# Feed-forward gate and linear blocks in three rounded passes, one rotated buffer, scale and shift on ScalarE, and new instruction orders in a six-layer attention stack

## The chip, the cores and the metric

The kernel runs on one core of one Trainium2 chip. The metric is the device time of one execution in microseconds (us). Engines are named as in the profile: PE is the matmul engine (PEld its weight loads), DVE the vector engine, ACT the activation engine, POOL GpSimd, SP the engine that issues the DMAs.

## The reference

`x` holds 128 sequences of 32 tokens with 128 features. A state-space block (`_L0_cond_ref`, not touched) gives the input of six layers, and the result of the six layers is added to `x`. A layer, with `shift` moving the second half of the features one token later:

```
y = shift(x) @ Wqkv                 # 128 -> 3 x 1024: q, k, v of 16 heads of 64
q, k = l2norm(q), l2norm(k)         # per head, times q_scale / k_scale
q, k = q*cos*s + rot(q)*sin*s, k*cos/s + rot(k)*sin/s
p = softmax(8 * q @ k.T, causal)    # 32 tokens of one sequence
x = x + (p @ v) @ Wo
n = layernorm(shift(x)) * g + b
a, gate = split(n @ W1 + b1)        # 341 columns each
x = x + (a * gelu(gate)) @ W2 + b2
```

## The kernel before

The 4096 tokens are 32 tiles of 128 tokens; four tiles are a group of 512 tokens, so a layer has 8 groups and the six layers 48. The residual `res` stays on chip as 128 features x 4096 tokens. Five instruction streams, one for each engine, are written by hand as a `body` that handles one group in four steps j = 0..3; semaphores join them. `group_steps` (L666) unrolls groups 0 and 1 of a layer and loops over groups 2 to 7. The work is staggered over the steps: in step n an engine works on projections and rotation of tile n, on transposes, key placement and `copy_v` of tile n-1, on scores and softmax of tile n-2, and on the weighted values of tile n-3. `project_out` of a group runs in step 3 of the next group, and the feed-forward of a group (`subtract_mean`, `variance`, three `gate_block`s, three `a_block`s, `down`) in steps 0 to 2 of the group after that.

Products with large weights are made in three passes over operands that are split in two rounded (fp32r) parts, high and low: high x high, high x low, low x high. The parts are made by an ACT copy to fp32r (`round_part` L1113, `round_wo` L1108, `copy_oT` L1039) and a subtraction on DVE or POOL (`rest_of_part`, `rest_of_wo`, `rest_of_outputs` L1253). The feed-forward blocks (L914, L925), the transposes (L819) and `down` (L932) work on plain fp32, and such a matmul of 512 columns stands in the trace as two instructions.

The order of a step on each engine is that of its `body`: PE L935, ACT L1122, DVE L1281, POOL L1403, SP L759. The parts that matter here:

- A query or key tile is squared by ACT into `sq` (L976, L983) and summed by DVE (`sum_squares` L1179). DVE multiplies it with cosine (`times_cos` L1186) and sine (L1195), POOL adds the two into `qk_r` (`rotate` L1347) and multiplies keys with the inverse norm (`norm_keys` L1356), PE transposes (L819), and ACT copies the transposes out of `px` (`copy_qT` L1023, `copy_kT` L1030). `qk_r` has two buffers, by the parity of the tile.
- `px` in PSUM is shared by both transposes and the weighted values, so `weigh_values` (L873), and the mask fill in front of it (L843), wait for `copy_kT`. `pg` is shared by all products of the feed-forward and by `project_out`.
- The feed-forward of a group: PE L896, ACT square and copy (L1087, L1094), PE L903, ACT logarithm and exponential (L1100, L1106), DVE `normalise` (L1243) at the end of step 0 and `scale_shift` (L1250) at the start of step 1. In step 1 three `gate_block`s alternate with `gate_gelu` (L1053), between two activation table loads (L1060). `gated` (L1235) of block k waits for `a_block` k, and `a_block` k+1 waits for it.
- At the end of a group's attention DVE adds `project_out` to the residual (`add_attention` L1267), ACT copies it shifted into `fs` (`shift_ffn` L1079), and only then comes ACT's `copy_oT` (L1045), for which DVE's `rest_of_outputs` (L1257) waits.
- In group 1 of a layer ACT rounds `Wo` in step 0 (L1111), and POOL makes its low part (`rest_of_wo` L1368) at the end of step 0.

## Time and profile before

| | us |
|---|---|
| median of 3 runs | 2977.76 (2974.36 to 2978.22) |
| profiled execution, own time | 2975.6 |
| its span, first to last instruction | 2973.8 |
| busy: PE / DVE / ACT / POOL | 2805.6 / 2630.3 / 2170.5 / 2129.8 |
| granted PE clock, mean | 0.984 |

The busy time of PE is a union of records whose ends are modelled; starts are the safer reading. The first 400 us are the state-space block and the start of the first layer; the last 50 us are the drain of the last groups and the final addition.

### The profile page before, as it was taken

How to read it: one execution, taken by the hardware profiler on the slowest of the kernel's cores; microseconds unless marked ns; L12 is line 12 of the kernel's file. 1: busy time of each engine (PE TensorE's matmuls, PEld its weight loads, DVE VectorE, ACT ScalarE, POOL GpSimd, SP SyncE). 2: the span in 40 equal slices, each digit the busy share in tenths (PEclk: the TensorE clock that was granted, in tenths of full speed). 3: DMA queues.
4: the chain of work that ended last, by engine and by line, in shares of the span. 5: the costliest groups of instructions: out<-in, count | busy, mean ns of one | idle time of the engine just before them, and what ended most of it. 6: DMA issues, size and time to landing. Idle time of an engine off the chain costs nothing. (4 is left out here: it accounts for less than half of the span.)

```text
span 2973.8 us, 90541 instructions
## 1 busy us (share of the span) xinstructions
PE 2805.6 (94%) x35360; PEld 2069.6 (70%) x35360; DVE 2630.3 (88%) x3407; ACT 2170.5 (73%) x3499; POOL 2129.8 (72%) x1523
## 2 busy tenths in 40 slices
PE   8799978999999999999999999999999999999986
PEld 7688856776767676666767667676667767676762
DVE  7899968999998998989999899999999898999982
ACT  5688857777777877777787777777687777768761
POOL 6776767777777777777777777777877777777760
PEclk9899999999999999999999999999999999999997
DMA  1000022222223222222222222222232322222222
GB/s 52 22 1 1 1 52 65 66 73 66 65 64 76 66 66 69 64 73 67 72 66 62 67 73 70 68 67 64 65 74 65 74 66 58 70 64 62 58 64 61
DMA packets 103837, 178.36 MB, mean 60 GB/s; under 512 B 29222, under 2 KB 52836, under 8 KB 103524
## 3 DMA queue, kind: packets, MB, share of 16 engines
q1 hardware_dynamic: 102500, 174.69, 23.7%
q8 instruction: 116, 1.90, 0.3%
q10 hardware_dynamic: 1152, 1.20, 0.1%
q14 instruction: 69, 0.57, 0.1%
HBM read 22.72 MB, written 2.10 MB: 8 GB/s over the span
## 5 line engine op out<-in xcount | busy, mean ns | idle before, releaser
L1347 POOL TENSOR_TENSOR spare<-spare,qk_t 128x1024 f32<-128x1024 f32 x384 | 909.6, 2390 | 29.1 <-POOL xs_lo L1333 8.1
L1356 POOL TENSOR_TENSOR spare<-spare,inv 128x1024 f32<-128x1024 f32 x192 | 366.6, 1909 | 329.9 <-ACT inv L1015 326.2
L791 PE MATMUL pa<-w_hi,xs_hi 128*128 128x512 f32 x1152 | 552.7, 480 | 10.5 <-DVE w_lo L1317 5.6
L1179 DVE TENSOR_REDUCE ss<-sq 128x16 f32<-128x1024 f32 x384 | 461.0, 1200 | 29.2 <-ACT sq L976 28.3
L1186 DVE TENSOR_TENSOR spare<-pa,rot 128x1024 f32<-128x1024 f32 x384 | 465.5, 1212 | 0.0
L1195 DVE TENSOR_TENSOR qk_t<-pa,rot 128x1024 f32<-128x1024 f32 x384 | 465.4, 1212 | 0.0
L791 PE MATMUL pa<-w_hi,xs_lo 128*128 128x512 f32 x1152 | 455.8, 396 | 0.0
L791 PE MATMUL pa<-w_lo,xs_hi 128*128 128x512 f32 x1152 | 454.4, 394 | 0.0
L819 PE MATMUL px<-ident_sb,spare 128*128 128x128 f32 x3072 | 410.3, 277 | 38.2 <-ACT qT L1023 32.3
L819 PEld LDWEIGHTS px<-ident_sb,spare 128*128 128x128 f32 x3072 | 339.7, 140 | 113.9 <-POOL spare L1356 59.0
L1363 POOL TENSOR_TENSOR sm<-sm,inv 128x512 f32<-128x512 f32 x192 | 201.3, 1048 | 258.0 <-DVE sm L1217 258.0
L1257 DVE TENSOR_TENSOR oT_lo<-px,oT_hi 128x1024 fp32r<-128x1024 f32 x192 | 228.6, 1191 | 120.9 <-ACT oT_hi L1045 120.8
L1030 ACT COPY k_both<-px 128x1024 f32<-128x1024 f32 x192 | 194.9, 1015 | 134.8 <-PE px L819 130.4
L791 PEld LDWEIGHTS pa<-w_hi,xs_hi 128*128 128x128 f32 x1152 | 218.3, 189 | 99.6 <-issue 57.9
L791 PEld LDWEIGHTS pa<-w_lo,xs_hi 128*128 128x128 f32 x1152 | 218.8, 190 | 76.1 <-issue 44.0
L983 ACT ACTIVATE sq<-pa 128x1024 f32<-128x1024 f32 x192 | 199.1, 1037 | 78.1 <-PE pa L791 76.1
L976 ACT ACTIVATE sq<-pa 128x1024 f32<-128x1024 f32 x192 | 196.8, 1025 | 80.3 <-PE pa L791 74.4
L791 PEld LDWEIGHTS pa<-w_hi,xs_lo 128*128 128x128 f32 x1152 | 217.7, 189 | 49.8
L853 PEld LDWEIGHTS ps<-kT,qT 128*32 128x32 f32 x12288 | 181.4, 110 | 99.3 <-issue 83.9
L873 PEld LDWEIGHTS px<-pT,spare 64*64 64x64 f32 x12288 | 198.2, 135 | 65.7 <-issue 64.4
L236 PE MATMUL c_bank<-c_h,c_cdiag 128*128 128x256 f32 x1024 | 231.6, 385 | 12.5 <-DVE c_h L530 11.6
L1023 ACT COPY qT<-px 128x1024 f32<-128x1024 f32 x192 | 194.0, 1011 | 48.3 <-PE px L819 48.3
(147 smaller groups left out, 5827.6 us busy)
## 6 DMA issues: line engine op xcount, KB each, us to landing
kT<-k_both SPq DMA_DIRECT2D x384, 256.0 KB, 3.7
pT<-prT SPq DMA_DIRECT2D x768, 64.0 KB, 2.0
w_part<-in_Wqkv SPq DMA_DIRECT2D x40, 192.0 KB, 3.7
wo<-in_Wo SPq DMA_DIRECT2D x6, 512.0 KB, 5.5
c_h<-in_x SPq DMA_DIRECT2D x4, 512.0 KB, 8.9
o_x<-in_x SPq DMA_DIRECT2D x8, 256.0 KB, 4.9
out<-o_out SPq DMA_DIRECT2D x8, 256.0 KB, 4.4
w<-in_W SPq DMA_DIRECT2D x6, 341.0 KB
```

The source lines that it names most:

```text
L236: last = pe.matmul(py[t % 2][:, 0:DI], cdiag[:, t % 3, n, :], h[:, t % 2, n, :], start=False, stop=(n == DS - 1))
L791: last = pe.matmul(pa[(u + c) % 2][:, half * 512:half * 512 + 512], x[:, j * P:(j + 1) * P], w[:, at], start=(k == 0), stop=(k == 2))
L819: last = pe.transpose(px[:, hp * P:(hp + 1) * P], qk_r[:, j % 2, c, hp * P:(hp + 1) * P], ident[:])
L873: last = pe.matmul(px[at:at + DH, to:to + 64], v[rows, j, h * DH:(h + 1) * DH], pT[rows, :, h, :], start=True, stop=True, skip_group_check ...
L983: act.activation(sq[:], pa[(3 * j + 1) % 2][:], ACT.Square).then_inc(s["sq_k"], 1)
L1179: dve.reduce_sum(ss[:, c, :], heads(sq[:]), AX.X).then_inc(s[sum_sem], 1)
L1186: dve.tensor_tensor(heads(qk_r[:, j % 2, c, :]), heads(pa[(3 * j + c) % 2][:]), per_head(rot[:, l % 2, 2 * c, :]), ALU.mult).then_inc(s[co ...
L1195: dve.tensor_tensor(halves(qk_t[:, c, :]), halves(pa[(3 * j + c) % 2][:])[:, :, ::-1, :], table.unsqueeze(1).to_broadcast([P, HEADS, 2, DH ...
L1257: dve.tensor_tensor(oT_lo[:, :, k, :].rearrange("p h (r q) -> p r h q", r=2), px[:].rearrange("p (r h q) -> p r h q", r=2, h=HP), oT_hi[:, ...
L1347: pool.tensor_tensor(qk_r[:, j % 2, c, :], qk_r[:, j % 2, c, :], qk_t[:, c, :], ALU.add)\
L1356: pool.tensor_tensor(k_r, k_r, over(inv[:, j % 2, 1, :], DH), ALU.mult).then_inc(s["norm_k"], 1)
L1363: pool.tensor_tensor(keys(sm[:]), keys(sm[:]), over(inv[:, j % 2, 0, :], S), ALU.mult)\
```

## The change

W1 is no longer kept in fp32: it is loaded into the storage of `wo` once `wo_lo` has been made, then split in `w1_hi` (ACT) and `w1_lo` (POOL). The normalised input is split into `fn_hi` (ACT) and `fn_lo` (DVE). Each gate or linear block is three matmuls of 512 columns in place of one in fp32. `scale_shift` moves from DVE to ACT. `qk_r` has one buffer, so `times_cos` waits for the transposes of the tile before and not of the one before that; `sq` and `k_both` move into the room that this frees. The orders of all four bodies change.

```diff
-        w1 = sb("w1", [DM, 2 * HID])
+        w1 = wo[:].rearrange("p h m -> p (h m)")[:, 0:2 * HID]
+        w1_hi = sb("w1_hi", [DM, 2 * HID], F32R)
+        w1_lo = sb("w1_lo", [DM, 2 * HID], F32R)
+        fn_hi = sb("fn_hi", [DM, GTOK], F32R)
+        fn_lo = sb("fn_lo", [DM, GTOK], F32R)
...
+                def load_w1(l):
+                    sp.wait_ge(s["wo_lo_ready"], l + 1)
+                    sp.dma_start(w1, of("W1", l)).then_inc(s["w1_loaded"], 16)
... SP body
                     for j in range(GT):
+                        if i % GROUPS == 1 and i < NG and j == 2:
+                            load_w1(i // GROUPS)
... PE gate_block; a_block likewise
-                            pe.wait_ge(s["fn_ready"], g + 1)
+                            pe.wait_ge(s["fn_lo_ready"], g + 1)
+                            pe.wait_ge(s["w1_lo_ready"], g // GROUPS + 1)
-                        pe.matmul(pg[0:m, :], w1[:, HID + at:HID + at + m], fx[:], start=True, stop=True)\
-                            .then_inc(s["gate_done"], 1)
+                        for p, (w, f) in enumerate(((w1_hi, fn_hi), (w1_lo, fn_hi), (w1_hi, fn_lo))):
+                            last = pe.matmul(pg[0:m, :], w[:, HID + at:HID + at + m], f[:], start=(p == 0), stop=(p == 2))
+                        last.then_inc(s["gate_done"], 1)
... PE body
                     for j in range(GT):
+                        project_q(i, j, l)
                         if j == 2:
                             a_block(i, 2, 1)
-                        project_q(i, j, l)
-                        if j == 0:
-                            subtract_mean(i, 2)
                         scores(i, j, 2)
                         transpose_q(i, j, 1)
+                        if j == 1:
+                            gate_block(i, 2, 0)
                         if j == 2:
                             a_block(i, 2, 2)
-                        if j == 1:
-                            gate_block(i, 2, 0)
+                        if j == 0:
+                            subtract_mean(i, 2)
                         project_k(i, j, l)
... ACT
+                def scale_shift(i, back):
+                        act.wait_ge(s["fn_mul"], g + 1)
+                        act.activation(fx[:], fx[:], ACT.Identity, scale=ln_par[:, 0:1], bias=ln_par[:, 1:2])\
+                            .then_inc(s["fn_ready"], 1)
+                def round_normed(i, back):
+                        act.wait_ge(s["fn_ready"], g + 1)
+                        act.copy(fn_hi[:], fx[:]).then_inc(s["fn_hi_ready"], 1)
+                def round_w1(l):
+                    act.copy(w1_hi[:], w1).then_inc(s["w1_hi_ready"], 1)
... ACT body
+                        if isinstance(g, int) and g == 1 and l < DEPTH and j == 3:
+                            round_w1(l)
                         copy_v(i, j, 1)
-                        square_q(i, j, 0)
                         log_norms(i, j, 1)
                         inverse_norms(i, j, 1)
+                        if j == 1:
+                            tables(i, 2, GELU)
+                        square_q(i, j, 0)
                         if j == 0:
                             shift_hi(i, 0, 1)
...
+                        if j == 2:
+                            shift_hi(i, -1, 0)
                         exponentials(i, j, 2)
                         if j == 3:
                             shift_ffn(i, 1)
+                        copy_oT(i, j, 3)
+                        if j == 0:
+                            scale_shift(i, 2)
+                            round_normed(i, 2)
+                        floor_norms(i, j, 0)
                         if j == 1:
                             round_part(l, g)
... DVE
-                        wait_for(dve, s[transposed], n - 1)
-                        dve.tensor_tensor(heads(qk_r[:, j % 2, c, :]), heads(pa[(3 * j + c) % 2][:]),
+                        wait_for(dve, s[transposed], n)
+                        dve.tensor_tensor(heads(qk_r[:, c, :]), heads(pa[(3 * j + c) % 2][:]),
+                def rest_of_normed(i, back):
+                        dve.wait_ge(s["fn_hi_ready"], g + 1)
+                        dve.tensor_tensor(fn_lo[:], fx[:], fn_hi[:].bitcast(F32), ALU.subtract).then_inc(s["fn_lo_ready"], 1)
... DVE body
                         if j == 1:
-                            scale_shift(i, 2)
-                        if j == 3:
-                            add_ffn(i, 2)
+                            rest_of_normed(i, 2)
+                        if j == 2:
+                            gated(i, 2, 1)
                         turn_probs(i, j, 3)
+                        maximum(i, j, 2)
                         sum_squares(i, j, 0, 0, "sq_q", "sum_q")
                         if j == 2:
                             gated(i, 2, 2)
-                        maximum(i, j, 2)
-                        times_sin(i, j, l, 0, "sq_q", "rot_q", "sin_q")
                         subtract_maximum(i, j, 2)
                         times_cos(i, j, l, 0, "sq_q", "tq_done", "cos_q")
+                        times_sin(i, j, l, 0, "sq_q", "rot_q", "sin_q")
                         times_sin(i, j, l, 1, "sq_k", "rot_k", "sin_k")
                         times_cos(i, j, l, 1, "sq_k", "tk_done", "cos_k")
-                        sum_squares(i, j, 0, 1, "sq_k", "sum_k")
                         if j == 1:
                             gated(i, 2, 0)
+                        if j == 0:
+                            normalise(i, 2)
+                        sum_squares(i, j, 0, 1, "sq_k", "sum_k")
                         denominators(i, j, 2)
                         if j == 3:
                             add_attention(i, 1)
-                        if j == 1:
-                            gated(i, 2, 1)
                         rest_of_outputs(i, j, 3)
-                        if j == 0:
-                            normalise(i, 2)
+                        if j == 2:
+                            add_ffn(i, 2)
... POOL
+                def rest_of_w1(l):
+                    pool.tensor_tensor(w1_lo[:], w1, w1_hi[:].bitcast(F32), ALU.subtract).then_inc(s["w1_lo_ready"], 1)
... POOL body
                     for j in range(GT):
-                        if j == 3:
-                            shift_lo(i, -1, 0)
-                        norm_keys(i, j, 1)
-                        if j == 3:
-                            rest_of_part(l, g)
                         norm_scores(i, j, 2)
...
                         norm_probs(i, j, 2)
+                        norm_keys(i, j, 0)
+                        if j == 2:
+                            shift_lo(i, -1, 0)
+                            rest_of_part(l, g)
                         if isinstance(g, int) and g == 1 and l < DEPTH and j == 0:
                             rest_of_wo(l)
+                        if isinstance(g, int) and g == 1 and l < DEPTH and j == 3:
+                            rest_of_w1(l)
```

## Rows read from the trace of the kernel before

**Rows 1.** Busy time per stretch: an ordinary group, and group 1 of a layer.

```profile
1536.00:1587.60 51.60, 50.05 (x700) 36.24 (x699) 47.09 (x55) 38.91 (x57) 38.36 (x25) 1.00 0.26 65
1690.60:1744.20 53.60, 50.37 (x700) 36.15 (x699) 48.72 (x56) 39.73 (x59) 42.20 (x32) 1.00 0.29 70
```

**Rows 2.** Waits, 400 to 2900 us: us in total, times, longest us.

```profile
DVE oT_lo L1257 <- ACT oT_hi L1045: 115.2, 47, 2.5
DVE gt L1235 <- PE pg L925: 63.4, 103, 0.9
PE ps L843 <- ACT k_both L1030: 37.7, 87, 1.3
```

**Rows 3.** ACT timeline in one group: start us, us, engine, line, operation [idle before <-releaser].

```profile
1546.37 0.32 ACT L1000 ACTIVATE over_floor<-ss,floor_c 128x32 f32<-128x32 f32 x1
1546.96 1.02 ACT L990 COPY spare<-pa 128x1024 f32<-128x1024 f32 x1 [0.27 <-PE pa L791]
1548.24 1.02 ACT L976 ACTIVATE sq<-pa 128x1024 f32<-128x1024 f32 x1 [0.27 <-PE pa L791]
1549.16 0.32 ACT L1007 ACTIVATE ln_ss<-over_floor,floor_c 128x32 f32<-128x32 f32 x1
...
1553.55 0.70 ACT L1053 ACTIVATE gt<-pg,b 128x512 f32<-128x512 f32 x1
1554.36 1.01 ACT L1030 COPY k_both<-px 128x1024 f32<-128x1024 f32 x1
```

**Rows 4.** Groups of instructions by line and shape: count, busy us, mean ns.

```profile
L1100 ACT ACTIVATE fx<-pg,eps_c 128x512 f32<-128x512 f32 x48 | 33.0, 688 | 3.4 <-PE pg L903 2.2
L1087 ACT ACTIVATE fx<-pg 128x512 f32<-128x512 f32 x48 | 28.7, 599 | 2.3 <-PE pg L896 1.2
L1120 ACT CAST w_hi<-w_part 128x384 f32 x30 | 14.9, 497 | 0.0
```

**Rows 5.** PE timeline in the same group.

```profile
1551.65 0.40 PE L791 MATMUL pa<-w_hi,xs_hi 128*128 128x512 f32 x1
...
1552.35 1.02 PE L914 MATMUL pg<-fx,w 128*128 128x512 f32 x2
1553.21 1.04 PE L819 MATMUL px<-ident_sb,spare 128*128 128x128 f32 x8
...
1557.02 1.13 PE L925 MATMUL pg<-fx,w 128*128 128x512 f32 x2
```

**Rows 6.** DVE timeline in the same group.

```profile
1538.21 1.22 DVE L1179 TENSOR_REDUCE ss<-sq 128x16 f32<-128x1024 f32 x1 [0.33 <-ACT sq L976]
...
1558.18 0.75 DVE L1235 SCALAR_TENSOR_TENSOR gt<-pg,b,gt 128x512 f32<-128x512 f32 x1
1558.85 0.68 DVE L1224 TENSOR_REDUCE den<-pr 128x16 f32<-128x512 f32 x1
1559.56 0.25 DVE L1227 RECIPROCAL rden<-den 128x16 f32<-128x16 f32 x1
1560.42 0.75 DVE L1235 SCALAR_TENSOR_TENSOR gt<-pg,b,gt 128x512 f32<-128x512 f32 x1 [0.61 <-PE pg L925]
...
1562.90 1.19 DVE L1179 TENSOR_REDUCE ss<-sq 128x16 f32<-128x1024 f32 x1
1564.79 0.75 DVE L1235 SCALAR_TENSOR_TENSOR gt<-pg,b,gt 85x512 f32<-85x512 f32 x1 [0.71 <-PE pg L925]
```

**Rows 7.** POOL timeline around step 1 of the same group.

```profile
1547.72 1.06 POOL L1381 TENSOR_TENSOR pr<-pr,rden 128x512 f32<-128x512 f32 x1
1549.97 1.91 POOL L1356 TENSOR_TENSOR spare<-spare,inv 128x1024 f32<-128x1024 f32 x1 [1.20 <-ACT inv L1015]
```

**Rows 8.** DVE and POOL timelines in group 1 of a layer.

```profile
1704.16 2.44 DVE L1250 TENSOR_SCALAR fx<-fx,ln_par 128x512 f32<-128x512 f32 x1
...
1703.96 2.35 POOL L1368 TENSOR_TENSOR wo_lo<-wo,wo_hi 128x1024 fp32r<-128x1024 f32 x1
```

**Rows 9.** `scale_shift` in the ordinary group, DVE timeline.

```profile
1548.94 0.55 DVE L1250 TENSOR_SCALAR fx<-fx,ln_par 128x512 f32<-128x512 f32 x1
```

More of the change, by code:

```diff
@@ L46 @@
 ROT_OPS = 6
-FFN_DMAS = 10
+FFN_DMAS = 9
 W_PART = 3 * INNER // GROUPS
@@ L612, in stack @@
         xs_lo = sb("xs_lo", [DM, GTOK], F32R)
-        sq = sb("sq", [P, INNER])
+        sq = spare[:, (GT + 2) * INNER:(GT + 3) * INNER]
         ss = sb("ss", [P, 2, HEADS])
@@ L617, in stack @@
         inv = sb("inv", [P, 2, 2, HEADS])
-        qk_r = spare[:, GT * INNER:2 * GT * INNER].rearrange("p (k c e) -> p k c e", k=2, c=2)
+        qk_r = spare[:, GT * INNER:(GT + 2) * INNER].rearrange("p (c e) -> p c e", c=2)
         qk_t = sb("qk_t", [P, 2, INNER])
@@ L621, in stack @@
         kT = sb("kT", [P, 2, HP, TILE_B, S])
-        k_both = sb("k_both", [P, HP * P])
+        k_both = spare[:, (GT + 3) * INNER:(GT + 4) * INNER]
         v = spare[:, 0:GT * INNER].rearrange("p (t c) -> p t c", t=GT)
@@ L767, in _ @@
                     if l + 1 < DEPTH and g == 4:
-                        sp.wait_ge(s["wo_lo_ready"], l + 1)
+                        sp.wait_ge(s["w1_lo_ready"], l + 1)
                         load_wo(l + 1)
@@ L818, in transposes @@
                     for hp in range(HP):
-                        last = pe.transpose(px[:, hp * P:(hp + 1) * P], qk_r[:, j % 2, c, hp * P:(hp + 1) * P], ident[:])
+                        last = pe.transpose(px[:, hp * P:(hp + 1) * P], qk_r[:, c, hp * P:(hp + 1) * P], ident[:])
                     last.then_inc(s[done], 1)
@@ L924, in a_block @@
                         at, m = HBLK[k]
-                        pe.matmul(pg[0:m, :], w1[:, at:at + m], fx[:], start=True, stop=True).then_inc(s["a_done"], 1)
+                        for p, (w, f) in enumerate(((w1_hi, fn_hi), (w1_lo, fn_hi), (w1_hi, fn_lo))):
+                            last = pe.matmul(pg[0:m, :], w[:, at:at + m], f[:], start=(p == 0), stop=(p == 2))
+                        last.then_inc(s["a_done"], 1)
                 def down(i, back):
@@ L975, in square_q @@
                         wait_for(act, s["sum_k"], n)
-                        act.activation(sq[:], pa[(3 * j) % 2][:], ACT.Square).then_inc(s["sq_q"], 1)
+                        act.activation(sq, pa[(3 * j) % 2][:], ACT.Square).then_inc(s["sq_q"], 1)
                 def square_k(i, j, back):
@@ L982, in square_k @@
                         act.wait_ge(s["sum_q"], n + 1)
-                        act.activation(sq[:], pa[(3 * j + 1) % 2][:], ACT.Square).then_inc(s["sq_k"], 1)
+                        act.activation(sq, pa[(3 * j + 1) % 2][:], ACT.Square).then_inc(s["sq_k"], 1)
                 def copy_v(i, j, back):
@@ L1029, in copy_kT @@
                         wait_for(act, s["kT_ready"], 32 * n)
-                        act.copy(k_both[:], px[:]).then_inc(s["tk_out"], 1)
+                        act.copy(k_both, px[:]).then_inc(s["tk_out"], 1)
                 def exponentials(i, j, back):
@@ L1139, in body @@
                         if j == 0:
+                            square_centred(i, 2)
                             copy_centred(i, 2)
```

46 lines of the change are left out of this document (21 added, 25 removed).

## The prediction

> **What bounds the kernel now.** I read the busy time per stretch first: an ordinary group takes 51.6 us, PE is busy for 50.05 of them and DVE for 47.09 [rows 1], at full clock (1.00, the 2.4 GHz level). The reader is to see that PE looks full and that 47.09 leaves DVE only 4.5 us. The waits say where those go: `oT_lo` waits for ACT 47 times, 2.5 us each, `gated` waits for PE 103 times [rows 2]. The 2.5 us are a fixed detour: after `add_attention` DVE waits until ACT has done `shift_ffn` and `copy_oT`. With them DVE is taken for 49.6 of 51.6 us. So the period is one chain through three engines, which I followed through the timelines. From `shift_ffn` to `copy_kT` of step 1 ACT runs nearly without idle time. PE is then released by `copy_kT` (mask, weighted values, `a_block` 0), and the three `a_block`s release the `gated`s. From the last `gated` (1564.79) DVE has no wait until `add_attention` 20 us later. What is worth time is what moves `copy_kT` of step 1, or the waits of `gated`, not the sum of PE's work.
>
> **Three passes for one fp32 block.** In [rows 5] three rounded passes take 0.70 us from start to start (1551.65 to 1552.35), the fp32 block behind them 0.86 (1552.35 to 1553.21). So a block gets 0.16 us shorter, six in a group: 0.9 us, 45 us over 48 groups, if PE alone set the period. It does not. The gate blocks stand in ACT's gaps in step 1 (gelu k releases gate k+1), and ACT is late there already. On the chain lies `a_block` 0 alone, 0.16 us.
>
> **ACT: two new instructions ahead of `copy_kT` of step 1.** `scale_shift` on ACT has no row. An activation of 512 columns takes 0.60 us, one with a column operand 0.69 [rows 4]; it has two, which at 0.09 each gives 0.78. Bounds: 0.60 and 0.9. It waits for `normalise`, which DVE now does before `sum_squares` of the keys, when `frs` has just been written; `copy_oT` stands before it on ACT, so I charge 0.03 for the wait. The rounding copy: 384 columns take 0.50 [rows 4], 512 with the same rate some 0.60; the next instruction starts about 0.1 before the end of a record (L1007 at 1549.16, before 1548.24 + 1.02) [rows 3], so 0.50. Together 1.31 (bounds 1.0 and 1.5).
>
> Against that stand ACT's present waits in this stretch. `copy_v` could start at 1546.60 and starts at 1546.96 (0.36, counted from where it could start, not from the record's end), `square_q` 0.38 late, `copy_kT` 0.21 late (1554.15 against 1554.36) [rows 3]: 0.95 that the later ACT absorbs. `copy_kT` then starts 1.31 - 0.95 = 0.36 later. Moving the table load and the two norm instructions ahead of `square_q` changes no sum on ACT; it only makes `square_q` of step 1 later, by about 3.4 us (it starts near 1550.8 + 0.9 for its end). DVE, which has by then done `rest_of_normed`, `turn_probs` and `maximum`, waits some 0.9 us for it, but reaches the end of `times_cos` of the keys at about 1558.1, ahead of `a_block` 0. So that wait costs nothing as long as `gated` 0 waits anyway, by 0.3 us.
>
> **DVE from `gated` 0 on.** `gated` 0 starts 1.16 after `a_block` 0 (1557.02 and 1558.18) [rows 5, 6]. After: 0.36 later, 0.16 earlier by the shorter block: 1558.38. `sum_squares` of the keys now comes after it, 1.1 us, so `denominators` start at 1558.38 + 0.67 + 1.11 = 1560.16, against 1558.85: 1.31 late. What goes are the waits of `gated` 1 (it could start at 1559.73, starts at 1560.42: 0.69) and of `gated` 2 (1564.00, 1564.79: 0.79) [rows 6]: `gated` 1 is moved behind `rest_of_outputs`, when `a_block` 1 has long been done (PE reaches it at about 1561, with `project_q` in front), and `gated` 2 behind `maximum`. 1.48 gone, 1.31 added: DVE is 0.17 us earlier at the end of the step, and nothing else waits up to `add_attention`. In step 0 `maximum` fills the wait for `square_q` (0.33) [rows 6], which in turn is 0.75 later by the order on ACT: even. A group is 51.4 us.
>
> **The rest of DVE.** `scale_shift` took 0.55 [rows 9]; `rest_of_normed` reads two SBUF tensors, and I take 0.7, the size of the PSUM-fed operations of 512 columns in `gated`; it lies before the wait for `square_q`, so 0.15 more is free. Bound: to 0.9 still free.
>
> **One buffer.** `times_cos` of a query now waits for the transposes of the tile before in the same step. PE does them right after `scores`, DVE reaches `times_cos` about 2 us after; for keys the margin is 2 us in steps 0 to 2 and some 0.9 us in step 3, where half of `project_out` stands before them. Cost 0; if the key margin goes, up to 0.5 us in step 3. Moving `norm_keys` from the start of the next step to the end of this one keeps POOL's cyclic order; POOL waits there for `inv`, which ACT now makes 0.9 us earlier. `shift_lo` and `rest_of_part` go ahead of `norm_scores` of step 3 either way.
>
> **Group 1 of a layer.** It takes 2.0 us more [rows 1]. One part is ACT's rounding of `Wo`, which stays (a copy of 128x1024, 1.0 us as L990 in [rows 3]). The other is `scale_shift`, which took 2.44 us in place of 0.55 in five of the 48 groups, because it started just after `rest_of_wo` on POOL (1703.96, 2.35) [rows 8, 9]. Then gate 0, the gelus and `copy_kT` were late by the other 1.0. POOL now does `norm_keys` first and `rest_of_wo` after it, and DVE's instruction comes before both. 5 x 1.0 = 5 us gained. The new W1 work is off the chain: `round_w1` (0.7, between the 0.60 of 512 columns and the 1.02 of 1024) stands in step 3, where ACT waits for PE (uncovered: 0.7 x 6 = 4 us); `rest_of_w1` (about 1.6) delays `norm_scores` of the next step 0, not needed for 1.5 us. `load_w1` on SP waits for `wo_lo_ready`, long set in step 2; a late one would hold `place_probs` behind it.
>
> **Sum.** 47 x 0.17 = 8, plus 5, less 1 in the drain, where the chain of the last group has two ACT hops more (1.4) and six shorter blocks (-0.9): 12 us. Profiled execution 2975.6 (span 2973.8, 1.8 around it) becomes 2964; the median stands 2.2 above it, so 2966.
>
> **A rule that speaks against it.** [rows 8] show a DVE instruction held until a POOL instruction ended. The Trainium skill ("SBUF — State Buffer", Who interferes with whom) says that a vector instruction with two SBUF inputs shares a read port with GpSimd exclusively: the second to come is blocked to the end of the first. The held one had a single tensor input, and `rest_of_normed` has two, so by that rule it inherits the same risk.
>
> **Rivals.**
>
> A. The port collision. `rest_of_normed` becomes ready at about 1548.9 to 1549.2 (end of `norm_probs`, now 1548.78 [rows 7]), `norm_keys` when ACT has made `inv`, about 1549.7. If `norm_keys` comes first, DVE waits 1.91 us [rows 7] in every group, gate 0 starts 2.2 us later, gelu 0 and `copy_kT` 1.4 later, since ACT had 0.8 to spare there. It decides from the point where DVE is 0.6 us later at `rest_of_outputs` of step 0. 48 x (1.4 - 0.17) = 59, less the 5 of the layers kept: 3020. For it: DVE is close. Against: `norm_keys` waits for ACT's `inv` (1.20 idle [rows 7]), and that is made behind the two new instructions. 0.15. By the skill's rule this is the case whenever the order flips, and by a rule of no contention it would be 2966 as well.
>
> B. PE and ACT are less tied than I read: the present waits of ACT in step 1 come from PE (`pa`), and shorter blocks shift PE earlier as well, so that `copy_kT` is not later. Then the 0.36 goes, and `gated` 0 is earlier until the end of `times_cos` (1558.1): 0.3 to 0.5 a group more. 2966 - 47 x 0.4 = 2947; with all 0.9 of PE gained, 2978 - 45 - 5 = 2928. For it: PE is 97% busy. Against: 87 waits of the mask for `copy_kT` [rows 2]. 0.22.
>
> C. Nothing is gained: the two ACT instructions cost 1.5 together, and 0.17 is eaten. 2978 - 5 + 1, or up to 10 more: 2974 to 2984. 0.18.
>
> **Chances.** Forecast 0.45 (its own range 2955 to 2973), A 0.15, B 0.22, C 0.18. About 0.2% (6 us) is what a measurement can tell from no change, that is 2972 to 2984. Faster: B, and 0.35 of the forecast's 0.45, since its 12 us are near the bound: 0.57. Same: the other 0.10 and 0.13 of C: 0.23. Slower: A and 0.05 of C: 0.20. The range 2932 to 2998 leaves out most of A and the far end of B.
>
> **What would show it.** Period between two L896-like centre products about 51.4, and 52.5 in group 1 of a layer. `gated` 1 and 2 without idle time before them, `gated` 0 with a short one for PE; a wait of about 0.9 us of `sum_squares` in step 1 for ACT. ACT's table load directly behind `inv`, `copy_kT` of step 1 0.3 to 0.4 later from `shift_ffn` than now. `rest_of_normed` at 0.7: if it stands at 2 us or more, A holds. The forecast is wrong if the mask's wait for `copy_kT` in step 1 grows beyond 0.8 us, or if DVE waits for `tk_done` in step 3.

## The result and the profile after

The changed kernel takes 2948.11 us (median of 5 runs, 2941.40 to 2949.14), the kernel before on the same chip 2978.22 us (5 runs, 2974.36 to 2981.80). The ratio is 0.9893, 95% interval 0.9882 to 0.9905: 30 us faster, about 1.1%. The forecast was 2966, 12 us faster. The sign and the mechanism held, the size did not. The profiled execution took 2947.82 us, 27.8 less than that of before (2975.6).

Busy time of the same two stretches, an ordinary group and group 1 of a layer, in the changed kernel (columns as in [rows 1]):

```profile
1520.24:1571.36 51.12, 48.70 (x702) 37.17 (x705) 46.87 (x55) 39.54 (x59) 38.42 (x25) 1.00 0.27 65
1673.61:1725.49 51.88, 48.72 (x701) 37.09 (x704) 46.90 (x56) 41.09 (x62) 42.25 (x32) 1.00 0.31 73
```

The ordinary group is 0.48 us shorter (51.60 in [rows 1]) and group 1 1.7 (53.60). PE has lost 1.35 us of busy time, ACT gained 0.6, DVE lost 0.2. DVE's waits, 400 to 2900 us, as in [rows 2]:

```profile
DVE oT_lo L1294 <- ACT oT_hi L1059: 122.7, 48, 7.7
DVE ss L1218 <- ACT spare L990: 72.9, 94, 3.2
DVE gt L1274 <- PE pg L938: 18.3, 44, 8.2
```

`gated` waited for PE 103 times (63.4 us); now it does 44 times, 18.3 us, of which one wait in the drain is 8.2. The detour over `oT_hi` is still there. New is the wait of `sum_squares` for ACT's squares (28.3 us in 50 waits before). ACT in step 1 of the ordinary group, as in [rows 3]:

```profile
1529.47 1.00 ACT L1059 CAST oT_hi<-px 128x1024 fp32r<-128x1024 f32 x1
1530.37 0.81 ACT L1127 ACTIVATE fx<-fx,ln_par 128x512 f32<-128x512 f32 x1
1531.29 0.62 ACT L1135 CAST fn_hi<-fx 128x512 fp32r<-128x512 f32 x1
1531.82 0.32 ACT L1014 ACTIVATE over_floor<-ss,floor_c 128x32 f32<-128x32 f32 x1
1532.04 0.99 ACT L1004 COPY spare<-pa 128x1024 f32<-128x1024 f32 x1
...
1533.62 1.28 ACT L1074 ACT_TABLE_LOAD   x1
1534.92 1.03 ACT L990 ACTIVATE spare<-pa 128x1024 f32<-128x1024 f32 x1
...
1538.78 1.05 ACT L1044 COPY spare<-px 128x1024 f32<-128x1024 f32 x1
```

None of these rows has idle time before it: the two new instructions took up the waits of 0.27 us seen in [rows 3]. PE's `a_block` 0 (first pass 1541.47) and what follows it, as in [rows 5]:

```profile
1541.47 0.50 PE L938 MATMUL pg<-fn_hi,w_hi 128*128 128x512 f32 x1
1541.81 0.40 PE L938 MATMUL pg<-fn_hi,w_lo 128*128 128x512 f32 x1
1542.05 0.40 PE L938 MATMUL pg<-fn_lo,w_hi 128*128 128x512 f32 x1
1542.28 0.40 PE L801 MATMUL pa<-w_hi,xs_hi 128*128 128x512 f32 x1
```

DVE from the end of step 0 on, as in [rows 6]:

```profile
1532.01 1.16 DVE L1294 TENSOR_TENSOR oT_lo<-px,oT_hi 128x1024 fp32r<-128x1024 f32 x1
1533.08 0.68 DVE L1288 TENSOR_TENSOR fn_lo<-fx,fn_hi 128x512 fp32r<-128x512 f32 x1
1533.69 0.70 DVE L1243 STREAM_TRANSPOSE prT<-pr 128x512 f32<-128x512 f32 x1
1534.32 0.65 DVE L1249 TENSOR_REDUCE top<-ps 128x16 f32<-128x512 f32 x1
1535.97 1.22 DVE L1218 TENSOR_REDUCE ss<-spare 128x16 f32<-128x1024 f32 x1 [1.01 <-ACT spare L990]
...
1542.48 0.75 DVE L1274 SCALAR_TENSOR_TENSOR gt<-pg,b,gt 128x512 f32<-128x512 f32 x1 [0.16 <-PE pg L938]
1543.15 1.21 DVE L1218 TENSOR_REDUCE ss<-spare 128x16 f32<-128x1024 f32 x1
...
1546.23 0.74 DVE L1274 SCALAR_TENSOR_TENSOR gt<-pg,b,gt 128x512 f32<-128x512 f32 x1
...
1549.21 0.73 DVE L1274 SCALAR_TENSOR_TENSOR gt<-pg,b,gt 85x512 f32<-85x512 f32 x1
```

`gated` 1 and 2 stand without idle time, `gated` 0 waits 0.16 us, `fn_lo` takes 0.68. Of the two signs by which the forecast would have been wrong, DVE waits for the transposes of the keys once, 0.3 us; the mask's own row is missing from this trace, so its wait can't be read.

Of the 27.8 us between the two profiled executions 25.4 lie in the 47 periods between one `shift_ffn` and the next, 1.7 ahead of them and 0.7 behind. Ordinary groups give about 0.5 each. The five periods that hold group 1 of layers 2 to 6 give 1.5 to 2.3 each, 9.6 together. The last period, in the drain, is 4.4 us *longer*, which hides part of the gain (below).

### The profile page after: what moved, and what is told of

Read it like the earlier page. It is cut to its first block and busy times, and to the rows that moved or that the text cites. A ratio compares the mean times of both kernels' runs of the same rounds, so it can differ in the third digit from the quotient of the medians.

```text
span 2946.0 us, 91092 instructions
## 1 busy us (share of the span) xinstructions
PE 2734.6 (93%) x35456; PEld 2117.2 (72%) x35648; DVE 2611.3 (89%) x3407; ACT 2208.1 (75%) x3601; POOL 2141.3 (73%) x1529
## 5 line engine op out<-in xcount | busy, mean ns | idle before, releaser
L1218 DVE TENSOR_REDUCE ss<-spare 128x16 f32<-128x1024 f32 x384 | 464.1, 1209 | 73.7 <-ACT spare L990 72.9
L801 PE MATMUL pa<-w_hi,xs_hi 128*128 128x512 f32 x1152 | 494.0, 429 | 13.5 <-DVE qk_t L1234 6.5
L1234 DVE TENSOR_TENSOR qk_t<-pa,rot 128x1024 f32<-128x1024 f32 x384 | 450.0, 1212 | 0.0
L883 PE MATMUL px<-pT,spare 64*64 64x64 f32 x12288 | 225.3, 222 | 97.8 <-ACT spare L1044 61.5
L1044 ACT COPY spare<-px 128x1024 f32<-128x1024 f32 x192 | 197.5, 1029 | 123.3 <-PE px L829 123.3
L1059 ACT CAST oT_hi<-px 128x1024 fp32r<-128x1024 f32 x192 | 193.5, 1008 | 85.5 <-PE px L883 84.3
L997 ACT ACTIVATE spare<-pa 128x1024 f32<-128x1024 f32 x192 | 199.4, 1039 | 74.2 <-PE pa L801 64.2
```

Of the source, the lines that this page charges most:

```text
L801: last = pe.matmul(pa[(u + c) % 2][:, half * 512:half * 512 + 512], x[:, j * P:(j + 1) * P], w[:, at], start=(k == 0), stop=(k == 2))
L883: last = pe.matmul(px[at:at + DH, to:to + 64], v[rows, j, h * DH:(h + 1) * DH], pT[rows, :, h, :], start=True, stop=True, skip_group_check ...
L997: act.activation(sq, pa[(3 * j + 1) % 2][:], ACT.Square).then_inc(s["sq_k"], 1)
L1218: dve.reduce_sum(ss[:, c, :], heads(sq), AX.X).then_inc(s[sum_sem], 1)
L1234: dve.tensor_tensor(halves(qk_t[:, c, :]), halves(pa[(3 * j + c) % 2][:])[:, :, ::-1, :], table.unsqueeze(1).to_broadcast([P, HEADS, 2, DH ...
```

## The experiments

Ratios are to the kernel before, with 95% intervals; medians in us. The kernel before took 2977.7 to 2979.8 beside fourteen of the versions, and 2976.2 beside the four that ran together (square_q first, rest_of_wo first, and the first two with scale_shift on ACT). "The changed kernel" is 2948; it was timed apart from the versions below, so small differences to it are read from the ratios and from the periods in the traces as well.

### Undoing parts of the change

**fp32 blocks again.** `square_centred`, which overwrites `fx`, now waits for the last `a_block` of the group before (`a_done`) and not for `fn_lo`, since PE reads `fx` itself. All else stays as changed.

```diff
-                        for p, (w, f) in enumerate(((w1_hi, fn_hi), (w1_lo, fn_hi), (w1_hi, fn_lo))):
-                            last = pe.matmul(pg[0:m, :], w[:, at:at + m], f[:], start=(p == 0), stop=(p == 2))
+                        last = pe.matmul(pg[0:m, :], w1_hi[:, at:at + m].bitcast(F32), fx[:], start=True, stop=True)
```

> The changed kernel with gate and linear blocks as one fp32 matmul again (the rounded W1 against the unrounded input; the low part of W1 and of the input are still made but not used). Theory 1 (the period is the chain ACT, a_block 0, gated): only the 0.16 us of a_block 0 and what gate blocks add to ACT's waits come back, 0.1 to 0.3 us a group: 5 to 14 us slower than the changed kernel, ratio to before about 0.992 to 0.994. Theory 2 (PE's busy time sets the period, the rival B of the prediction): all six blocks count, 0.9 to 1.0 us a group, 40 to 48 us slower, ratio 1.003 to 1.006, all of the gain lost.

2960.75, ratio 0.9944 [0.9930, 0.9958]: 12.6 us more than the changed kernel, 0.27 a group. The passes save 0.9 us of PE in a group, and less than a third of it reaches the time. PE is not the bound.

**`gated` 1 back at the end of step 1.**

```diff
-                        if j == 2:
-                            gated(i, 2, 1)
                         turn_probs(i, j, 3)
...
+                        if j == 1:
+                            gated(i, 2, 1)
                         rest_of_outputs(i, j, 3)
```

> The changed kernel with gated of block 1 back at the end of step 1. Theory 1 (the removed waits of gated on PE are what was gained): gated 1 waits for a_block 1 again, about 0.5 us, and that comes on top of the group: 51.1 becomes 51.5 us, 15 to 25 us slower than the changed kernel. Theory 2 (PE sets the period): PE runs ahead of DVE anyway and nothing changes, within 5 us.

2985.97, 1.0036 [1.0022, 1.0049]: 38 us more, above what was expected. The waits of that kernel show why:

```profile
PE px L829 <- DVE oT_lo L1294: 49.4, 48, 1.1
DVE gt L1274 <- PE pg L938: 40.7, 90, 0.7
```

DVE's 0.7 us wait before `gated` 1 is back, and the low part `oT_lo` behind it is late as well, on which PE's transposes of the next step wait 1.0 us in each group.

**The table load behind `square_q`.**

```diff
-                        if j == 1:
-                            tables(i, 2, GELU)
                         square_q(i, j, 0)
+                        if j == 1:
+                            tables(i, 2, GELU)
```

> The changed kernel with square_q of step 1 ahead of the gelu table load. DVE's wait of 1.0 us before sum_squares of step 1 goes. Theory 1 says that this wait is free, because gated 0 behind it waits for a_block 0 by 0.16 us: no change, within 4 us of the changed kernel. If DVE set the period: up to 1.0 us a group, 40 us faster.

2942.08 (4 runs, three at 2941.6 to 2942.4 and one at 2947.91), 0.9888 [0.9872, 0.9903]; the period is 51.15 us, as changed (51.12). DVE's 1.0 us wait for the square goes and comes back whole at `gated`:

```profile
DVE gt L1274 <- PE pg L938: 67.6, 48, 6.4
DVE ss L1218 <- ACT spare L990: 27.5, 48, 3.2
```

So that wait was free, as the prediction had it.

**`square_q` ahead of the norms and the table load on ACT.**

```diff
+                        square_q(i, j, 0)
                         log_norms(i, j, 1)
                         inverse_norms(i, j, 1)
                         if j == 1:
                             tables(i, 2, GELU)
-                        square_q(i, j, 0)
```

> The changed kernel with square_q ahead of the two norm instructions and the table load on ACT. Theory (the order on ACT is worth nothing by itself): 2945 to 2951. Rival (it carries the 0.3 us a group that were measured beyond the forecast): 2960 to 2965.

2949.01, 0.9910 [0.9896, 0.9923]: the rival falls. The order is worth little, but not nothing: `copy_kT` of step 0 stands at 8.76 us after the start of `shift_ffn`, for 8.66 in the changed kernel, and the period is 51.21 us for 51.12, some 4 us in all. The last period of this execution is 3.3 us shorter than in the changed kernel's profile, which hides it; the ratio, 5 us above that of the changed kernel, agrees with it.

**`rest_of_normed` behind `maximum`,** where it becomes ready beside POOL's `norm_keys`.

```diff
-                        if j == 1:
-                            rest_of_normed(i, 2)
                         if j == 2:
                             gated(i, 2, 1)
                         turn_probs(i, j, 3)
                         maximum(i, j, 2)
+                        if j == 1:
+                            rest_of_normed(i, 2)
```

> The changed kernel with rest_of_normed two instructions later on DVE (about 1.2 us), when norm_keys of POOL has begun. If an instruction of DVE with two SBUF inputs is held by POOL's (the port rule, rival A): rest_of_normed takes 2.0 us in place of 0.68, gate block 0 starts 2.4 us later, and copy_kT of step 1 is about 1.4 to 1.6 us later: 55 to 75 us slower than the changed kernel. If not: it takes 0.68, gate block 0 is 1.2 us later, of which ACT absorbs most; 0 to 20 us slower.

3049.21, 1.0238 [1.0224, 1.0253]: 101 us more than the changed kernel, beyond the expectation. One `fn_lo` and the POOL instruction that runs when it starts, in that kernel:

```profile
1522.56 1.90 POOL L1393 TENSOR_TENSOR spare<-spare,inv 128x1024 f32<-128x1024 f32 x1 [0.54 <-ACT inv L1029]
1523.36 1.64 DVE L1288 TENSOR_TENSOR fn_lo<-fx,fn_hi 128x512 fp32r<-128x512 f32 x1
```

Its 1.64 us end 0.54 us after POOL's instruction ends (1524.46); undisturbed it takes 0.68 in all. Later start and hold together push `gated` 0 from 24.53 to 26.0 us after the group's start and the period from 51.12 to 52.59. This is rival A, made to happen: 60 us over the ordinary groups, and 67 with the five of group 1, within the expectation, as is `copy_kT` of step 1, 1.5 us later.

The rest comes from the clock. PE waits 1.84 us for `fn_lo` ahead of gate block 0, and in 20 of the 46 groups ahead of the drain the granted clock then falls to the 1.2 GHz level for 3.4 us, which it does in none of them in the changed kernel. One such group, the PE timeline and 3.3 us of it (columns as in [rows 1]):

```profile
1525.06 0.50 PE L926 MATMUL pg<-fn_hi,w_hi 128*128 128x512 f32 x1 [1.84 <-DVE fn_lo L1288]
...
1526.54 0.63 PE L801 MATMUL pa<-w_hi,xs_lo 128*128 128x512 f32 x1
1526.97 0.63 PE L801 MATMUL pa<-w_hi,xs_hi 128*128 128x512 f32 x1
```

```profile
1526.20:1529.50 3.30, 3.30 (x9) 2.48 (x8) 2.80 (x3) 2.47 (x3) 2.38 (x3) 0.50 0.01 3
```

A pass takes 0.43 us from start to start there, for 0.23 at full clock. Ordinary groups with such a stretch take 54.16 us, those without it 52.59, a difference of about eight passes at 0.2 us more each; over 20 groups that is 31 us. With the 67 it makes up the 97 us between the two profiled executions. The hold itself is what the Trainium skill says ("SBUF — State Buffer", Who interferes with whom) of a DVE instruction with two SBUF inputs; the trace agrees.

**`rest_of_wo` ahead of `norm_keys`.**

```diff
                         norm_probs(i, j, 2)
+                        if isinstance(g, int) and g == 1 and l < DEPTH and j == 0:
+                            rest_of_wo(l)
                         norm_keys(i, j, 0)
```

> The changed kernel with rest_of_wo ahead of norm_keys in group 1 of a layer. Theory (the gain of group 1 is the hold that went): rest_of_normed starts behind rest_of_wo and is held by it in five groups; these get 1 to 2 us longer, 2953 to 2958. Rival (the gain came from scale_shift being off DVE): 2948.

2947.59, 0.9895 [0.9882, 0.9908]: no difference that the runs can tell. In the trace the two instructions meet, but the other way round:

```profile
1686.41 0.68 DVE L1288 TENSOR_TENSOR fn_lo<-fx,fn_hi 128x512 fp32r<-128x512 f32 x1
```

```profile
1686.50 2.84 POOL L1409 TENSOR_TENSOR wo_lo<-wo,wo_hi 128x1024 fp32r<-128x1024 f32 x1
```

DVE came 0.09 us first and keeps its 0.68; POOL's instruction takes 2.84 in place of the 2.40 it has in the changed kernel. So who is held is decided by who comes first, here by 0.09 us. POOL's delay costs little: four of the five periods are 0.33 us longer than in the changed kernel. Since the hold of the theory did not occur, this run does not decide between the two causes of group 1's gain; the one with `rest_of_wo` moved in the kernel before (below) does.

### Adding parts to the kernel before

**One rotated buffer alone** (the wait of `times_cos` changed with it).

```diff
-        qk_r = spare[:, GT * INNER:2 * GT * INNER].rearrange("p (k c e) -> p k c e", k=2, c=2)
+        qk_r = spare[:, GT * INNER:(GT + 2) * INNER].rearrange("p (c e) -> p c e", c=2)
```

> The kernel before with one buffer for rotated queries and keys, nothing else. The prediction's claim, cost 0: times_cos comes 2 us (queries) and 0.9 to 2 us (keys) after the transposes that it now waits for; within 3 us of before. The rival: in step 3, behind half of project_out, the keys' times_cos waits, 0.5 us a group, 20 to 25 us slower.

2979.57, 1.0002 [0.9993, 1.0011]: nothing, as predicted.

**`rest_of_wo` moved from the end of step 0 to behind `norm_keys` of step 1.**

```diff
-                        if isinstance(g, int) and g == 1 and l < DEPTH and j == 0:
-                            rest_of_wo(l)
...
                         norm_keys(i, j, 1)
+                        if isinstance(g, int) and g == 1 and l < DEPTH and j == 1:
+                            rest_of_wo(l)
```

> The kernel before with POOL's rest_of_wo behind norm_keys of the next step, so that scale_shift of DVE is not held by it in group 1 of five layers. Prediction: gate 0, the gelus and copy_kT are 1.0 us earlier there, 5 us faster in all. From the trace after, where these groups gained 1.5 to 2.3 us and not 0.5 + 1.0: up to 9 us faster. If the hold is hidden by ACT's own lateness: 0.

2971.80, 0.9980 [0.9971, 0.9989]: 6.5 us. The five periods with group 1 lose 0.5 to 1.7 each; `scale_shift` is no longer held by `rest_of_wo` as in [rows 8].

**DVE's order around `gated`,** and nothing else.

```diff
+                        if j == 2:
+                            gated(i, 2, 1)
                         turn_probs(i, j, 3)
+                        maximum(i, j, 2)
                         sum_squares(i, j, 0, 0, "sq_q", "sum_q")
                         if j == 2:
                             gated(i, 2, 2)
-                        maximum(i, j, 2)
...
-                        sum_squares(i, j, 0, 1, "sq_k", "sum_k")
                         if j == 1:
                             gated(i, 2, 0)
+                        sum_squares(i, j, 0, 1, "sq_k", "sum_k")
...
-                        if j == 1:
-                            gated(i, 2, 1)
```

> The kernel before with DVE's new places of gated, maximum and sum_squares alone (fp32 blocks, scale_shift on DVE, two buffers and all other orders as before). Theory 1 (the gain is the two waits of gated that go, the rest of the change nets to nothing): gated 0 at the same place, 0.5 us a group from there on, 20 to 27 us faster than before. Theory 2 (the gain needs the shorter PE blocks): gated 1 and 2 find PE late again, 0 to 8 us faster.

2962.97, 0.9946 [0.9933, 0.9960]: 15.3 us, half of the whole gain, from new places for `gated`, `maximum` and `sum_squares` on DVE. That lies between the two theories, below the 20 to 27 us of the first. What stays of DVE's waits for PE:

```profile
DVE gt L1235 <- PE pg L925: 51.3, 48, 9.9
DVE top L1210 <- PE ps L853: 46.4, 49, 3.6
```

The second is new: `maximum`, now early, waits 1 us in each group for `scores`. In the changed kernel this wait is 3.4 us in total.

**The last two together.** The edit is the sum of both.

> The kernel before with the two edits that were run alone, DVE's order and rest_of_wo behind norm_keys. If they are independent: 15.3 + 6.5 = 22 us faster than before, 2956; the other 8 us of the change's 30 are then in the three passes, the rounding and ACT's order together. If they share a wait: 15 to 18 us.

2958.25, 0.9938 [0.9926, 0.9950]: 21.6 us by the medians, 18.5 (15 to 22) by the ratio, so the times alone don't rule out a shared wait. The traces do: up to the last period, in the drain, the two alone shorten the periods by 17.6 and 5.3 us, together by 21.9. They add, nearly.

**And parts of ACT's order** (norms ahead of `square_q`, `square_centred` behind `copy_qT`).

```diff
-                        square_q(i, j, 0)
                         log_norms(i, j, 1)
                         inverse_norms(i, j, 1)
+                        square_q(i, j, 0)
...
-                        if j == 0:
-                            square_centred(i, 2)
...
                         copy_qT(i, j, 1)
                         if j == 0:
+                            square_centred(i, 2)
                             copy_centred(i, 2)
```

> As b4, with ACT's logarithm and inverse of the norms ahead of square_q and square_centred behind copy_qT, still with fp32 blocks and scale_shift on DVE. In the trace after, copy_kT of step 0 came 0.15 us earlier from shift_ffn than before; if that is the order alone, it shows here, and 0.15 x 47 = 7 us are gained on b4, 2949, as much as the whole change. If it needs the shorter PE blocks or scale_shift moved: within 3 us of b4.

3015.45, 1.0127 [1.0111, 1.0143]: 57 us slower than the version before it, a miss. DVE and POOL in that kernel, and the group of `scale_shift`:

```profile
1564.80 0.67 DVE L1242 TENSOR_TENSOR fx<-fc,pg 128x512 f32<-128x512 f32 x1
1565.59 2.00 DVE L1249 TENSOR_SCALAR fx<-fx,ln_par 128x512 f32<-128x512 f32 x1
1567.51 0.70 DVE L1203 STREAM_TRANSPOSE prT<-pr 128x512 f32<-128x512 f32 x1
```

```profile
1564.36 1.09 POOL L1380 TENSOR_TENSOR pr<-pr,rden 128x512 f32<-128x512 f32 x1
1565.37 1.94 POOL L1355 TENSOR_TENSOR spare<-spare,inv 128x1024 f32<-128x1024 f32 x1
```

```profile
L1249 DVE TENSOR_SCALAR fx<-fx,ln_par 128x512 f32<-128x512 f32 x48 | 93.2, 1941 | 5.2
```

ACT makes `inv` 0.9 us earlier, so `norm_keys` starts at 1565.37, 0.22 ahead of `scale_shift`, which then takes 2.00 us in place of 0.55 [rows 9], in nearly every group (mean 1.94). The changed kernel has these two orders on ACT without harm; here they cost 57 us. The next four runs test that reading.

**`scale_shift` on ACT, with ACT's new order and with the old one.** Fp32 blocks, no rounding, on the last two versions.

```diff
                         copy_oT(i, j, 3)
+                        if j == 0:
+                            scale_shift(i, 2)
```

> The version with the DVE, POOL and ACT orders on fp32 blocks, and scale_shift moved from DVE to the end of step 0 on ACT; no rounding of the input, no three passes. Theory (the 57 us came from scale_shift held by norm_keys): scale_shift costs 0.8 us on ACT and cannot be held; 2955 to 2965, a period of 51.2 to 51.5 us. Rival (the order on ACT itself costs it, square_q too late in step 1): 3000 or more.

> The version with the DVE and POOL orders, with scale_shift on ACT and the order on ACT otherwise that of before. Theory (ACT's waits of 0.95 us between the group's start and copy_kT of step 1 absorb 0.8): 2954 to 2962, as without it. Rival (a later ACT is passed on in full): 0.7 x 47 = 33 us more, 2991.

3105.49, 1.0432 [1.0419, 1.0445], and 3107.57, 1.0435 [1.0422, 1.0449]. Both expectations missed: I had left `normalise` at the end of DVE's step 0. ACT in the first:

```profile
1541.76 1.00 ACT L1045 CAST oT_hi<-px 128x1024 fp32r<-128x1024 f32 x1
1545.78 0.81 ACT L1113 ACTIVATE fx<-fx,ln_par 128x512 f32<-128x512 f32 x1 [3.02 <-DVE fx L1252]
```

ACT stands 3.0 us in every group, and the period is 54.9 us (53.94 in ordinary groups at full clock, 55.09 in the 22 in which the granted clock falls to the 1.2 GHz level for 3.4 us: some 27 us in all are the clock's). So the change's own place of `normalise`, to which the prediction gave half a sentence, is needed as soon as `scale_shift` is on ACT. With it moved ahead of `sum_squares` of the keys:

```diff
+                        if j == 0:
+                            normalise(i, 2)
                         sum_squares(i, j, 0, 1, "sq_k", "sum_k")
```

> As the version with scale_shift on ACT, the new ACT order and the DVE and POOL orders on fp32 blocks, and now normalise ahead of sum_squares of the keys on DVE. Theory (normalise's place made ACT wait 3.0 us in the run before; the place, ACT's instruction and ACT's order belong together): the wait goes, 2955 to 2965, a period of 51.2 to 51.5 us. Rival (the order on ACT itself costs it): 3000 or more.

> The same with the order on ACT of before. Theory (ACT's waits of 0.95 us absorb the 0.8 of scale_shift; the order on ACT is worth nothing): 2954 to 2964, within 3 us of the run beside it. Rival (the new order on ACT is needed to keep copy_kT of step 1 in place): 10 to 30 us above the run beside it.

2966.15, 0.9958 [0.9944, 0.9972], and 2967.17, 0.9965 [0.9952, 0.9979]. ACT's order makes no difference once `scale_shift` cannot be held: 3015 falls to 2966 by moving `scale_shift` and `normalise`. The rival falls. Both are about 8 us above the version with the DVE and POOL orders: `copy_kT` of step 1 comes 0.3 us later (20.99 against 20.68 after the group's start), so `scale_shift` on ACT costs something, and was not wholly absorbed as expected.

### More work on ACT, and a further move

**`copy_centred` in two halves,** some 0.6 us more on ACT, in the changed kernel.

```diff
-                        act.copy(fc[:], pg[:]).then_inc(s["fc_ready"], 1)
+                        act.copy(fc[0:64, :], pg[0:64, :])
+                        act.copy(fc[64:P, :], pg[64:P, :]).then_inc(s["fc_ready"], 1)
```

> The changed kernel with copy_centred of step 0 as two copies of half the partitions, 0.5 us more on ACT ahead of copy_kT of step 0. Theory 1 (from shift_ffn to copy_kT of step 1 ACT is the chain): 0.4 to 0.5 us a group, 20 to 25 us slower than the changed kernel, 2965 to 2973. Theory 2 (PE or DVE alone sets the period, ACT has 25% idle): within 5 us.

2976.22, 0.9994 [0.9985, 1.0003]: 28 us more than the changed kernel, somewhat above the expectation. `copy_kT` of step 1 comes 0.7 us later and the period is 0.7 longer: behind it nothing is left to absorb. ACT up to there is on the chain.

**`shift_hi` of step 0 behind the last gelu,** to unload that stretch, and then `normalise` one place earlier. In both, POOL's `shift_lo` of step 1 moves behind the first `rotate` (not shown below).

```diff
-                        if j == 0:
-                            shift_hi(i, 0, 1)
...
                             gate_gelu(i, 2, 2)
+                            shift_hi(i, 0, 1)
```

> The changed kernel with shift_hi of the second half (0.82 us of ACT) taken out of step 0 and put behind gelu 2 of step 1, and POOL's shift_lo between the two rotates of step 1. ACT's chain from shift_ffn to copy_kT of step 1 is 0.82 shorter, but scale_shift then waits for DVE's normalise, which is not earlier: of 0.82 some 0.3 remain, 14 us faster than the changed kernel, 2934 (bounds 0 and 38). If ACT's chain does not set the period: within 4 us.

```diff
+                        if j == 0:
+                            normalise(i, 2)
                         times_cos(i, j, l, 1, "sq_k", "tk_done", "cos_k")
```

> As c1, with DVE's normalise of step 0 ahead of times_cos of the keys, so that scale_shift does not wait: 0.6 to 0.8 us a group, 28 to 38 us faster than the changed kernel, 2910 to 2920. If c1 gives as much already, normalise was not the wait, and c2 equals c1.

2964.27, 0.9955 [0.9942, 0.9968], and 2957.66, 0.9929 [0.9915, 0.9942]: 16 and 10 us slower than the changed kernel, two misses. `copy_kT` comes earlier, at 20.64 and 20.32 (20.83 as changed), but later steps lose more than that: `xs_lo`, which POOL now makes later, is waited for by the projections (32.8 us in the second), and DVE waits for POOL's late `norm_probs` (22.5 us). None of the variants is measurably faster than the changed kernel; the table-load variant equals it in period.

## Why the prediction was right or wrong

**The chain was right.** ACT from `shift_ffn` to `copy_kT` of step 1, PE's `a_block` 0, DVE to the end of the group: adding to ACT moves the period by the same amount (0.7 for 0.7), shortening PE by 0.9 moves it by 0.27, and DVE's new order around `gated` gives half of the gain.

**The step that failed is the sum of the ordinary group: 0.17 us predicted, 0.49 measured.** Its terms had the right sign. Two were mis-sized, both to the same side: ACT's delay of `copy_kT` (0.36 predicted, 0.19 measured), and what DVE gains behind `gated` 0 (0.37 predicted, 0.56 measured). Between the two points 0.04 go the other way. Times from the start of `shift_ffn`, medians over the ordinary groups:

| point | before | after | predicted shift | measured |
|---|---|---|---|---|
| `copy_kT`, step 1 | 20.64 | 20.83 | +0.36 | +0.19 |
| `gated` 0 | 24.46 | 24.53 | +0.20 | +0.07 |
| period | 51.61 | 51.12 | -0.17 | -0.49 |

- ACT's two new instructions cost what was worked out: `over_floor` starts 1.32 later behind `copy_oT`'s start of step 0 than before (1.31 predicted; `scale_shift` 0.81 for 0.78, rounding 0.62 for 0.60). They absorb 1.03 us and not 0.95, and 0.11 us were gained ahead of them in step 0, most of it where `shift_hi` now starts 0.10 before its forerunner (`square_q`) ends, and only 0.02 before when that was `inv`. "Changes no sum on ACT" overlooked that.
- DVE from `gated` 0 on gained 0.56 for 0.37. The two waits (1.48 predicted, 1.47 found) and `sum_squares` (1.11, 1.13) were right. The rest are small gaps not counted: `turn_probs` followed `rest_of_outputs` 0.09 us later than need be, as it waited for POOL, and `add_ffn` 0.06 later; the others are of 0.01 to 0.02 us each, behind `gated` and `maximum`. Why these went was not tested. Over 47 groups 0.02 us is already 1 us.
- The three passes, put at 0.16 us a group, are no part of this shortfall, though putting fp32 blocks back costs 0.27. `gated` 0 starts 1.00 us after `a_block` 0 for 1.16 before, as predicted. In the changed kernel with fp32 blocks `gated` 0 comes 0.08 us later (24.61). The other 0.19 come behind it: `copy_kT` of steps 2 and 3 is 0.4 us later than in the changed kernel, and DVE's `times_cos` of the keys in step 3 starts 0.15 us later behind its forerunner:

```profile
1517.44 1.03 PE L829 MATMUL px<-ident_sb,spare 128*128 128x128 f32 x8
```

```profile
1518.59 1.22 DVE L1223 TENSOR_TENSOR spare<-pa,rot 128x1024 f32<-128x1024 f32 x1
```

  PE's transposes end at 1518.47, 0.12 before DVE starts. That is the key margin of the one buffer, which the prediction priced at 0 with "up to 0.5 us in step 3" if it went. In the versions with fp32 blocks and two buffers that gap is not there. So the passes keep that margin open, and buffer and passes are not two independent prices; alone on the kernel before, the buffer cost nothing. No run had the changed kernel with fp32 blocks and two buffers, so this is read from the traces and not isolated.

**Group 1 of a layer** gave 1.5 to 2.3 us over five periods, of which about 0.5 is the ordinary gain: some 7 us for the 5 predicted. The mechanism, a `scale_shift` held by `rest_of_wo`, is borne out: moving POOL's instruction away in the kernel before gave 6.5 us, and all five holds went (`scale_shift` at 0.55). In the changed kernel the old place of `rest_of_wo` costs next to nothing, but only because DVE's `rest_of_normed` comes 0.09 us ahead of it.

The new work for `W1` stayed off the chain, as forecast: `round_w1` takes 0.75 us six times (0.7 predicted), and the five periods that hold it and group 1's other work are 0.7 us longer than an ordinary one, for 0.8 in the version with the DVE and POOL orders, which has no `round_w1`.

**The drain** was put at +1 (its two terms, 1.4 and -0.9, give 0.5). In the profiled execution the last period is 4.4 us longer than before, but in the table-load variant 1.2 shorter. The clock tells them apart; these are 40 us of the drain, the changed kernel and then that variant:

```profile
2860.00:2900.00 40.00, 27.81 (x241) 16.65 (x242) 11.82 (x17) 10.35 (x13) 3.15 (x3) 0.66 0.09 22
```

```profile
2860.00:2900.00 40.00, 24.88 (x244) 14.04 (x244) 11.75 (x18) 12.52 (x17) 3.15 (x3) 0.80 0.08 21
```

In these 40 us the granted clock stood at the 1.2 GHz level for 27.3 us in the first and for 15.8 us in the second. The profiles of all versions go the same way: the eight in which the clock is at that level for 20 us or more of the last period have last periods of 48.0 to 50.4 us, the other twelve, that of the kernel before among them (6.8 us), of 43.1 to 48.0. Runs of one kernel fall on either side: 2941.4 and 2947.8 to 2949.1 of the changed one, 2941.6 and 2947.9 of the variant. That the clock takes some 6 us there in most runs of the changed kernel is read from profiles, not isolated by an experiment; the median's gain of 30 contains it, and what the clock takes from the median of the kernel before is open.

**Rival A** did not happen, and is real. `rest_of_normed` starts 0.67 us ahead of `norm_keys` (1533.08 against 1533.75): the prediction's 0.6 us of margin was about right. Its price was worked out wrong: 1.4 - 0.17 a group, less 5, gives 54 us, which counts from the kernel before (3032), but was added to the forecast, which has the 0.17 and the 5 in it already (3020). Crossed, it costs 1.47 us a group at full clock, near the 1.4 of the working, though here the instruction also starts two places later; with group 1 that is some 67 us, and the lower clock in 20 groups, which the prediction did not have, brings it to 101. It explains why the parts don't add: -20 for the DVE and POOL orders, +57 for parts of ACT's order while `scale_shift` is on DVE, and no measurable difference when it isn't. **Rival B's** outcome (2947) was closer than the forecast, by luck: its first half, `copy_kT` hardly later, holds in part, but its cause, PE's shorter blocks pulling ACT forward, does not: with fp32 blocks `copy_kT` stands at 20.76, and not later. **Rival C** is refuted. One reading was off without harm: `square_q` of step 1 starts 2.4 us later in the group and not 3.4, where the start of before was compared with the end of after; the wait of DVE for it is 1.0 us, for the 0.9 predicted.

**Sum.** From 2978: DVE and POOL orders -20, `scale_shift` and `normalise` moved with either ACT order +8, the three passes -13. That leaves -5 for the remaining orders (PE's, which takes away `maximum`'s wait of 1 us; POOL's `norm_keys` and `shift_lo`) less what the split of the input costs on ACT and DVE. These weren't separated, and each of these terms carries an error of some us.

## What to carry to other kernels

Where one chain runs through three engines, price a shorter instruction by its place on the chain: 0.9 us of PE a group were worth 0.27. Look first for instructions that wait in line while others behind them are ready; new places for `gated` and two others gave half of the gain. Where a DVE instruction on SBUF operands runs near a POOL one, find which comes first and by how much: here margins of 0.2 to 0.7 us decided over 57 and 67 us, so orders on *other* engines that make POOL ready earlier have to be costed too. Before the whole of a loss is put down to a wait, compare the granted clock of the groups: of the 101 us here, some 31 were the clock's.

## What was not expected of the hardware

- The hold between DVE and POOL goes both ways and needs no second tensor input on DVE: `scale_shift` (one tensor input, fp32, SBUF to SBUF) took 2.00 us for 0.55 when POOL had started 0.22 us before it; `fn_lo` 1.64 for 0.68 when POOL had started 0.80 before it; POOL's `wo_lo` 2.84 for 2.40 when DVE had started 0.09 before it.
- Not to be seen as holds are POOL's rotations beside DVE's `times_cos` and `times_sin`, which read PSUM and SBUF: all 384 of each take 1.21 to 1.23 us in the changed kernel.
- With `rest_of_normed` behind `maximum`, PE's wait of some 1.84 us before gate block 0 was followed by 3.4 us at the 1.2 GHz level in 20 groups, and not in others with the same wait. Each such stretch made the group 1.57 us longer.
- In the last period the granted clock was at its lower level for 27.3 us in one profile and for 10.2 us in another of nearly the same program. What decides between them stays open.
